# Four of eight expert rows summed by TensorE with diagonal weight matrices, and later gathers

## The reference

```python
x = x + L0_xattn(layernorm(x), ctx_2048, ...)
x = x + L0_ffn(layernorm(x), W_router, W_gate, W_up, W_down)   # 64 experts, top 8
x = x + L1_xattn(layernorm(x), ctx_2048, ...)
x = x + L1_ffn(layernorm(x), ...)                              # 64 experts, top 8, capacity 128
```

```python
comb = sum(one_hot(top_idx) * top_w[..., None], axis=1)
out = einsum('eti,eih->th', silu(g) * u * comb.T[:, :, None], W_down)   # = sum over 8 k of w[k] * y[k]
x   = x + out
```

## Time and profile before

| | |
|---|---|
| profiled execution | 2035.62 us |
| its span (first to last instruction) | 2033.8 us |
| runs | 2036.14, 2037.71, 2038.18 us |
| TensorE busy | 1634.2 us (80%) |
| VectorE busy | 1412.9 us (69%) |
| ScalarE busy | 1230.3 us (60%) |
| GpSimd busy | 986.1 us (48%) |
| granted TensorE clock, mean | 0.951 |
| DMA | 390.94 MB, mean 192 GB/s |

### The profile page before, as it was taken

The page is one execution under the profiler, slowest core; times in us unless marked ns, Lnnn a source line. Parts: engine busy times, 40 slices in busy tenths (PEclk is TensorE's granted clock), DMA queues, the critical chain, the costliest instruction groups (busy, mean ns, idle before and its releaser), DMA issues. The chain is left out here.

```text
span 2033.8 us, 44372 instructions
## 1 busy us (share of the span) xinstructions
PE 1634.2 (80%) x12470; PEld 1095.2 (54%) x12623; DVE 1412.9 (69%) x4341; ACT 1230.3 (60%) x3174; POOL 986.1 (48%) x1114
## 2 busy tenths in 40 slices
PE   3999999999974999999997278888888888855551
PEld 1555555555543889888886134444444444444430
DVE  5888899999954445545434489999999999743330
ACT  1777777777752566666665268778878777621110
POOL 4367777777763000000001776666666662158883
PEclk9999999999986999999999589999999999979996
DMA  5688878777757976666665678887877775178856
GB/s 141 159 211 249 240 215 217 214 216 213 207 159 225 289 213 202 195 200 198 196 199 169 163 188 219 224 224 198 202 193 195 197 198 144 49 198 185 176 93 112
DMA packets 413085, 390.94 MB, mean 192 GB/s; under 512 B 46640, under 2 KB 385072, under 8 KB 412848
## 3 DMA queue, kind: packets, MB, share of 16 engines
q1 hardware_dynamic: 346496, 265.28, 49.2%
q0 software_dynamic: 37904, 90.22, 16.9%
q10 hardware_dynamic: 28448, 32.59, 5.5%
HBM read 233.74 MB, written 170.16 MB: 199 GB/s over the span
## 5 line engine op out<-in xcount | busy, mean ns | idle before, releaser
L1125 DVE TENSOR_REDUCE mx<-psS 128x2 f32<-128x512 f32 x1024 | 679.0, 674 | 86.5 <-PE psS L1518 59.0
L923 ACT ACTIVATE prob<-psE 128x512 f32<-128x512 f32 x1024 | 594.4, 591 | 235.8 <-PE psE L1531 219.2
L772 POOL DMA_INDIRECT yg<-y_d,row_all x256 | 248.4, 970 | 630.8 <-SPq L413 480.0
L1531 PE MATMUL psE<-q,k 128*128 128x256 bf16 x2048 | 394.1, 275 | 30.7 <-issue 10.2
L1518 PE MATMUL psS<-k,q 128*128 128x512 bf16 x871 | 336.5, 388 | 27.0 <-DVE mx L1125 14.1
L1470 DVE TENSOR_TENSOR hid<-sil,psE 128x96 f32<-128x96 f32 x384 | 97.7, 254 | 331.0 <-ACT sil L1024 331.0
L1643 PE MATMUL psE<-wt,xgT 128*128 (+1 forms) x1536 | 323.9, 335 | 2.1 <-ACT xgT L1019 1.6
L759 POOL DMA_INDIRECT xs_d<-xr,row_all x256 | 251.5, 982 | 94.4 <-ACT prob L923 46.1
L1531 PEld LDWEIGHTS psE<-q,k 128*128 128x128 bf16 x2048 | 187.1, 98 | 181.3 <-ACT prob L923 62.6
L1549 PE MATMUL psO<-prob,v 128*32 128x256 f32 x4096 | 275.0, 386 | 0.0
L1019 ACT COPY xgT<-psS 128x256 f32<-128x256 f32 x384 | 144.6, 376 | 186.7 <-PE psS L1637 160.7
(11 more groups left out here) (220 smaller groups left out, 2539.0 us busy)
## 6 DMA issues: line engine op xcount, KB each, us to landing
xg<-xs_d SPq DMA_DIRECT2D x320, 128.0 KB, 2.6
y_d<-y_all SPq DMA_DIRECT2D x320, 128.0 KB, 2.3
q<-q_stack_d SPq DMA_DIRECT2D x128, 256.0 KB
k<-k_stack_d SPq DMA_DIRECT2D x128, 256.0 KB
wt<-in_gu ACTq DMA_DIRECT2D x110, 192.0 KB, 2.9
q_stack_d<-parts SPq DMA_DIRECT2D x64, 192.0 KB
k_stack_d<-parts SPq DMA_DIRECT2D x64, 192.0 KB
wt<-in_dn ACTq DMA_DIRECT2D x110, 96.0 KB, 3.6
```

Source lines behind the costliest of these rows:

```text
L772: g.indirect_dma_start(yg[:, k, :], None, y0_d[:, :], bass.IndirectOffsetOnAxis(row_all[:, row(st.pair("load") * K + k, 1)], 0))\
L923: a.activation(prob[gr][:, u % 4, :], psE[ring][:, :], ACT.Exp, scale=SCALE).then_inc(s_exp, 1)
L1125: v_.tensor_reduce(mx[b][:, bg // 4, :].rearrange("p (h r) -> p h r", h=2)[:, :, (bg % 4) * 2 + tt], psS[(UNITS * (st.s0 - LAG["smax"]) + ...
L1531: ins = m_.matmul(psE[ring][:, i * T:(i + 1) * T], k2[b][:, bg, hh * T + i * P:hh * T + (i + 1) * P], q2[b][:, bg, :], start=True, stop=True)
```

## The change

ScalarE no longer weights the rows 0 to 3. One step earlier (steps 5 to 31, units 0 to 3) it makes four diagonal 128 x 128 matrices, the identity times a token's weight (`diag`, two buffers). TensorE multiplies each with the gathered row block and accumulates the four in PSUM (`weigh`, in units 4, 5, 5 and 6, behind the scores of the unit and ahead of K, OT0 and OT1), in columns 256 to 511 of `psO`. `values` therefore uses columns 0 to 255 alone, for both halves. VectorE's additions `two` and `one` are gone; its `add_row`s move to units 4, 5, 6, 7, and `x2` to unit 8, where it reads PSUM. GpSimd's gathers move from paces 2 to 9 to 5, 6, 7, 8, 9, 11, 12, 14; `remainder` now comes behind the fifth of them and `third_part` behind the seventh. Steps before 6 keep their sum.

```diff
-PACE = (..., (2, 3, 4, 5, 6, 7, 8, 9))
+PACE = (..., (5, 6, 7, 8, 9, 11, 12, 14))
-ADDED, TWO, ONE, ALL, MOMENTS = (4, 5, 7, 8), 6, 7, 9, (10, 11)
+ADDED, ALL, MOMENTS = (4, 5, 6, 7), 8, (10, 11)
+WEIGHTED = (4, 5, 5, 6)
...
+        def weighted(s0, n):
+            return 4 * (s0 - FULL) + n
 # gather, GpSimd
-                        if k < 4:
+                        if k < 4 and st.s0 >= FULL:
+                            hold(pool, s_wsum, weighted(st.s0, k + 1))
+                        elif k < 4:
 # body, GpSimd, steps from FULL
-                        for k in range(K):
+                        for k in range(5):
                             gather(st, k, PACE[L][k])
+                        remainder()
+                        for k in (5, 6):
+                            gather(st, k, PACE[L][k])
+                        third_part()
+                        gather(st, 7, PACE[L][7])
 # ScalarE
-                    a.copy(osb[:, half, :], psO[:, half * T:(half + 1) * T]).then_inc(s_oev, 1)
+                    a.copy(osb[:, half, :], psO[:, 0:T]).then_inc(s_oev, 1)
...
+                    if L == 1 and u in PRODUCTS and FULL - 1 <= st.s0 < PAIRS:
+                        k, t = PRODUCTS.index(u), st.s0
+                        if k == 0:
+                            wait(act, s_wsum, weighted(st.s0 - 1, 0))
+                        a.mul(diag[t % 2][:, k, :], ident[:, :], w_all[:, t * K + k:t * K + k + 1]).then_inc(s_diag, 1)
-                    if L == 1 and u in products and st.on("comb"):
+                    if L == 1 and u in products and st.on("comb") and st.s0 < FULL:
 # sums, VectorE
+                        if st.s0 >= FULL:
+                            dve.wait_ge(s_wsum, weighted(st.s0, 4))
+                            dve.wait_ge(s_pv, st.n("attn", 4, 1))
+                            four = psO[:, T:2 * T]
...
-                        v_.tensor_tensor(x2[b][:, :], ys[:, 0, :], ys[:, 4, :], ALU.add).then_inc(s_x2, 1)
+                        v_.tensor_tensor(x2[b][:, :], four, ys[:, 4, :], ALU.add).then_inc(s_x2, 1)
 # values, TensorE
+                    if st.L == 1 and q == 1 and st.s0 >= FULL and st.on("comb"):
+                        pe.wait_ge(s_x2, st.n1("comb"))
...
+                def weigh(k):
+                    if k == 0:
+                        pe.wait_ge(d_yg[0], st.n1("comb", 16 * 4))
+                        pe.wait_ge(s_diag, weighted(st.s0, 4))
+                        pe.wait_ge(s_oev, st.n("back", 2))
+                    m_.matmul(psO[:, T:2 * T], diag[(st.s0 - LAG["comb"]) % 2][:, k, :], yg[:, k, :],
+                              start=(k == 0), stop=(k == 3)).then_inc(s_wsum, 1)
...
+                    if L == 1 and st.on("comb") and st.s0 >= FULL:
+                        for k in range(4):
+                            if WEIGHTED[k] == u:
+                                weigh(k)
```

More of the change, by code:

```diff
@@ L91 @@
 NB = 3
-PACE = ((6, 8, 10, 12, 14, 0, 2, 4), (2, 3, 4, 5, 6, 7, 8, 9))
+PACE = ((6, 8, 10, 12, 14, 0, 2, 4), (5, 6, 7, 8, 9, 11, 12, 14))
 AT_ONCE = 5
@@ L100 @@
 PRODUCTS = (0, 1, 2, 3)
-ADDED, TWO, ONE, ALL, MOMENTS = (4, 5, 7, 8), 6, 7, 9, (10, 11)
+ADDED, ALL, MOMENTS = (4, 5, 6, 7), 8, (10, 11)
+WEIGHTED = (4, 5, 5, 6)
 def units_of_products(s0):
-    if s0 >= FULL:
-        return PRODUCTS
     return (12, 13, 14, 15) if s0 == FULL - 2 else (8, 9, 10, 11)
@@ L111, in units_of_sum @@
     if s0 >= FULL:
-        return ADDED, TWO, ONE, ALL, MOMENTS
+        return ADDED, None, None, ALL, MOMENTS
     if s0 == FULL - 1:
@@ L327, in build @@
         yg = ab("yg", [P, K, T])
-        ys = ab("ys", [P, K, T])
+        ys = ab("ys", [P, 5, T])
+        diag = [ab(f"diag{b}", [P, 4, P]) for b in range(2)]
         zf = xr[0]
@@ L396, in build @@
         s_sum, s_match = sem("s_sum"), sem("s_match")
+        s_diag, s_wsum = sem("s_diag"), sem("s_wsum")
         s_chain = sem("s_chain")
@@ L841, in body @@
                             gather(st, k, 0)
-                    remainder()
-                    third_part()
+                    if st.s0 < FULL:
+                        remainder()
+                        third_part()
                     if st.s0 < FULL - 1:
@@ L1194, in sums @@
                     if u == all_:
-                        ch.join("one")
                         dve.wait_ge(s_sum, st.n1("comb", 4))
                         wait(dve, d_x2[b], st.nbuf1("comb") - 16)
-                        v_.tensor_tensor(x2[b][:, :], ys[:, 0, :], ys[:, 4, :], ALU.add).then_inc(s_x2, 1)
+                        if st.s0 >= FULL:
+                            dve.wait_ge(s_wsum, weighted(st.s0, 4))
+                            dve.wait_ge(s_pv, st.n("attn", 4, 1))
+                            four = psO[:, T:2 * T]
+                        else:
+                            ch.join("one")
+                            four = ys[:, 0, :]
+                        v_.tensor_tensor(x2[b][:, :], four, ys[:, 4, :], ALU.add).then_inc(s_x2, 1)
                     if u == moments[0]:
@@ L1546, in values @@
                         wait(pe, s_oev, st.n(stage, 2, half))
+                    if st.L == 1 and q == 1 and st.s0 >= FULL and st.on("comb"):
+                        pe.wait_ge(s_x2, st.n1("comb"))
                     for i in range(2):
                         for j in range(4):
-                            ins = m_.matmul(psO[32 * j:32 * j + 32, half * T:(half + 1) * T],
+                            ins = m_.matmul(psO[32 * j:32 * j + 32, 0:T],
                                             v[b][:, i, unit_at(4 * q + j), :], prob[gr][:, j, i * T:(i + 1) * T],
```

## The result

The changed kernel takes 2069.79 us (median of 4 runs, 2067.84 to 2070.77), the kernel before 2037.95 in the same comparison (4 runs, 2036.14 to 2044.08). The ratio is 1.0149, with a 95% interval of 1.0132 to 1.0166: some 32 us slower. The forecast was 2034.1 us, with a range of 2026 to 2047.

What follows compares the result with a forecast made beforehand. VectorE was taken to bound the step, with a loop through TensorE; 0.2 us gained in 23 steps (4.6) less 1.0 lost in steps 6 to 9 gave 3.6, from 2037.7 to 2034.1 us, range 2026 to 2047.

Steps and rivals of the forecast that it cites:

- the part on GpSimd, SyncE and the DMA: Gathers wait for later units, third_part 1.4 us later, gather 7 lands in 3 us; nothing waits, priced at 0.
- VectorE's saving: Additions two and one go: VectorE spared 0.93 us a step, of which 0.21 shortens the step.
- TensorE's chain: Four weigh products at 0.43 us each, 1.72 a step, three ahead of scores 6; Q starts 0.12 us later.
- a PSUM source: For x2 reading PSUM, 0.01 us taken; the skill's rule gave 0.065 us, 1.3 us less gain in total.
- A: VectorE's saving falls fully through because the weighs fill TensorE's waits: 12.6 us gained, 2025 us; chance 0.15.
- B: TensorE's chain becomes the bound, each weigh costing 0.60 us instead of 0.43: 2046 us; chance 0.22.
- C: Gather 7 lands late, in 4.2 us instead of 3, and VectorE's first add_row waits: 2050 us; chance 0.12.
- D: Nothing moves, the step being held elsewhere, such as ScalarE's run of units 8 to 15: within 1 us of 2037.7; chance 0.11.
- wrong if the step is longer than 19.1: Sign on step length: about 18.9 us expected, forecast wrong if longer than 19.1 or shorter than 18.7 us.

Runs made afterwards that it cites:

- f1_third_earlier: The changed kernel with third_part moved to stand behind gather 5 instead of gather 6; 2040.53 us, ratio 1.0011.
- g1_third_on_mask: The kernel before, with third_part in layer 1 waiting for VectorE's second addition to id_acc, two operations ahead of mask; 2070.96 us, ratio 1.0155.
- g4_gathers_alone: The kernel before with only the changed kernel's gather paces and order of gathers, remainder and third_part; 2061.36 us, ratio 1.0108.
- f0_changed: The changed kernel run again without an edit; 2073.27 us, ratio 1.0174.
- f3_fill: The changed kernel with seven more products, results unused, in TensorE's wait ahead of V; 2057.33 us, ratio 1.0108.
- g2_gathers_soon: The changed kernel with the old gather paces 2 to 9, remainder between gathers 6 and 7, third_part behind all gathers; 2037.14 us, ratio 0.9993.
- g3_weighs_spread: The kernel of g2_gathers_soon with the four weigh products in units 4, 5, 6, 7 instead of 4, 5, 5, 6; 2026.36 us, ratio 0.9932.
- the f's: Follow-up runs of the changed kernel unedited, with third_part earlier or products added, and of the kernel before with third_part held; kernel before 2037.57 us there.
- the g's: Follow-up runs with third_part held onto mask, the gathers' part alone, gathers sooner, or weighs spread; kernel before 2038.67 us there.
- the e's: First four follow-up runs, on a slower chip: third_part earlier, gathers alone, third_part held, products added in TensorE's wait; kernel before 2132.87 us there.

## Why the prediction was wrong

**The step that failed** is the part on GpSimd, SyncE and the DMA: "put `third_part` at about 1513.4, 1.4 later ... I price this at 0". The move itself was right: 12.36 us behind the maximum of unit 4 before (1499.65 to 1512.01), 13.69 after, 1.33 later. I asked who waits for its result and never what runs beside it. `mask` stood half a microsecond behind its end, and my own figures put the new one, 1513.4 to 1514.6, on top of a `mask` at about 1513.5. The rows leave `mask` out, but one late `third_part` with a `mask` of 0.51 stood in the same trace. The price was +0.90 in each step (shown by `f1_third_earlier`, which takes it away, and `g1_third_on_mask`, which makes it alone). On the path it is worth 1:1, because VectorE has no gap in units 9 to 3, as the prediction itself says.

The Trainium skill (SBUF — State Buffer, section "SBUF: two separate sides") gives a reason. A pair of SBUF ports is shared by VectorE and GpSimd as an exclusive lock; a VectorE operation with two SBUF inputs and a GpSimd operation that reads SBUF shut each other out, for the whole of the one that starts first. The traces agree in three places (the changed kernel, `g1_third_on_mask`, `g4_gathers_alone`): `mask` (inputs `rest` and `logit`) ends 0.08 to 0.10 behind `third_part` whatever moment of it `mask` started in. They do not agree on who goes first: in `g4_gathers_alone` the `mask` of 1365.53 starts ahead of `third_part` and takes 1.77 us, where by the page it would have had the ports first. Starts recorded for GpSimd are rough, so this stays open. No run here looks at the ports themselves; that they are the cause is the page's word.

**The second loss had no step in the prediction.** I noted the clock at 1.00 and dropped it. The longer `mask` lengthened TensorE's wait ahead of V by as much (1.11 to 1.97), and behind such waits the clock fell in 8 steps, 11 in `f0_changed`, 1.67 us each: 13 to 18 us. `f3_fill` shows that this part hangs on TensorE's idle time. Why one wait of 1.97 is followed by a low stretch and the next is not stays open; in the kernel before, with 1.45, none was, nor behind the single waits of 1.92 and 1.93 in `f1_third_earlier`, `g2_gathers_soon` and `g3_weighs_spread`.

**What held.** VectorE's saving and TensorE's chain: a `weigh` has 0.43 to the next start (1502.36 to 1502.79 in the changed kernel), Q is 0.16 later (forecast 0.12), the wait ahead of the maximum of unit 8 is 0.88 (1.0), unit 10 is 0.24 earlier (0.21), and with `mask` out of the way the step is 18.91 (18.9). `x2` with one input from PSUM takes 0.41 us (median 411 ns, 417 before), so what the Trainium skill (VectorE: DVE Perf Modes, the section on the TRN2 errata) gives for a PSUM source, and what I had left out of the sum, has no part in it. ScalarE is busy 1222.4 us instead of 1230.3, and no loss was traced to it.

**The rivals.** A did not come, but its numbers were right for another placing (`g3_weighs_spread`). B is refuted by the 0.43 and by `f1_third_earlier`. C did not decide (the changed kernel's sums wait 15.1 us for `yg`, 13.5 before), but is there in small once the step is short: 7.9 us in `f1_third_earlier`, where gather 7's record of 1.55 instead of 0.95 adds to it. D did not come: the step moved. My signal "wrong if the step is longer than 19.1" was the one that fired, at 19.76.

The range did not hold the time because all its cases were waits for a result. A GpSimd operation moved onto one of VectorE's, and a clock that falls, were in none of them.

## What to carry to other kernels

When an operation of GpSimd or VectorE moves, lay its new time over the other engine's timeline, and look at every operation with two SBUF inputs that it will then overlap. In these traces such a pair (two `TENSOR_TENSOR`s) held one another, although nothing in the program connects them and no row shows a wait, only a longer duration. The longest duration in a source view is the place to look: 508 ns beside a median of 225 would have told it here. If VectorE is the bound, put GpSimd's long operations beside VectorE's reads of PSUM: in the kernel before, a maximum at 1512.44 took its usual 0.65 inside `third_part`. And when a step grows, look at what TensorE's longest wait becomes: here its clock took 13 to 18 us, about as much as the longer step itself.

## What the hardware showed that I had not expected

- A `TENSOR_TENSOR` of 128x64 took 0.22 to 0.23 us alone, 0.73 half-way into GpSimd's, 1.13 to 1.18 at its start, and up to 1.77 when its record began ahead of it, always until just behind GpSimd's end.
- It goes the other way too: in `f1_third_earlier` the gather issued at 1519.68 has 1.55 us instead of 0.95, beside VectorE's `hotr` (two inputs, 1519.19 to 1520.40). The gather ahead of it, which was running when `hotr` began, kept its 0.96, and `hotr` took 1.21, as it does beside no gather at all (`g1_third_on_mask`, at 1513.40).
- The kernel before has this loss in every steady step, off the path: the last operation of `roots`, on 128 x 2 numbers, took 1.03 us at the median beside `hotr` (1514.44 to 1515.66), and 0.19 in the changed kernel, where it stands clear of it.

```profile
1514.70 1.01 POOL L790 TENSOR_TENSOR rstd<-below,rstd 128x2 f32<-128x2 f32 x1
```

- TensorE at 2.4 GHz with one wait of about 2 us in 20 fell to 1.2 GHz for 3.4 us in some steps, though it was busy 88% of the time around; seven products in that wait, whose results nobody reads, kept the clock up and were worth 16 us.
- The same kernel takes 2038 us in the comparisons of the result, the f's and the g's, and 2133 on the chip of the e's, and the order of two variants can turn round between them.
